# State-space and expert layer: a chunk's products as 64x64 quadrants, y's channels reordered, three of eight gathered pieces without the add

## The chip, the cores and the metric

One core of a Trainium2 chip runs the whole kernel in one launch. The metric is the device time in microseconds (us), from profiled and unprofiled executions of the same program.

## What is computed

The input x has 32 sequences of 256 tokens, 128 channels (8192 tokens). Every token is normalised to xn, and the output is `x + ssm(xn) + ffn(xn)`.

- `ssm` projects xn to 256 hidden channels, mixes them by a gate with a convolution of three tokens, and runs a linear recurrence with 16 states per channel along the sequence: `state = A_d * state + B_d * u_t`, `y_t = sum(state * C)`. Then `out = y @ W_out.T + b_out`, and the result is a layer norm of `xn + out` with gain and offset.
- `ffn` is a mixture of eight experts (128 to 512 to 128, relu). Each token goes to two neighbouring experts, and the two outputs are averaged.

## The kernel before, in words

All engines run programs written out by hand, joined by semaphores. The order is: statistics and normalising; projections, while GpSimd (POOL) scatters the tokens to DRAM in expert order; 37 tiles of 256 sorted tokens through two experts each, their outputs stored in `ys_dram`; the state-space loop; the output projection with the last layer norm. The change touches the last two stages and one small thing at the start.

**State-space loop** (TensorE, L1277 to L1316; VectorE, L1096 to L1104; ScalarE, L707 to L724). The recurrence is cut into chunks of Q = 32 tokens, 256 chunks in all. One group g holds four hidden channels, whose 4 x 32 tokens are the 128 partitions; the 256 chunks are the columns. 64 groups (32 for each half `hb` of the hidden channels) are taken as 32 pairs r, and two pairs make a duo q; there are 16 duos (`NDUO`). For a duo PE runs three phases of fp32 matmuls:

- `inject(q + 1)` (L1287): what each chunk adds to the 64 states of a group, a 128x64 weight, 224 columns, four matmuls; the two groups of a pair (`ab`) go to PSUM partitions 0 to 63 and 64 to 127 of bank `q % 2`.
- the products inside the chunk (L1307): a 128x128 weight `INTRA[:, g, :]`, 256 columns, four matmuls. This weight is block diagonal, four blocks of 32x32, one for each channel; the rest is zero.
- the read-out of the states (L1313): 64 rows by 128 columns, 256 columns, four matmuls, accumulated on the products inside. It waits for the scan of the duo on VectorE (`s_scan`, L1102).

The scan needs `inject`, and the decay rows that ScalarE writes (`decay`, L712). ScalarE moves each pair's result from two PSUM banks to SBUF over the inputs u (L723). Six banks hold three pairs. In the second half of the loop (q from 8, `DPB`) VectorE also transposes the finished first half of y after each scan, in eight pieces of 1024 tokens (`y_piece(0, n)`, L1093; `YT[0]` is `RC[:, 1, :]`).

**Output stage.** After the last duo VectorE runs `y_piece(1, 0)` and `y_piece(1, 1)`, and then a written-out sequence over 16 groups of 512 tokens: `stats`, `scale_batch`, `y_piece(1, n)`, `gain(n)` (L1138) and `add_base(n)` (L1143) for the eight pieces n; after `add_base(n)` SP stores piece n (L462). PE projects y with `WoT` (L1328), whose rows have to be in the channel order of y's partitions.

**Gathers.** `add_base(n)` adds `GA[n]`, which is x plus the expert outputs in token order. SP first loads x into `GA[n]` (`load_x`, L434); POOL waits for it and issues eight indirect DMAs of 128 rows each with an add at the destination (L548). `GA[0..3]` lie in `AR`, which is free once the experts are done; `GA[4..7]` lie over `INTRA`'s first half and are loaded after pair 16. Their order on POOL is n = 0 to 7, 64 DMAs in all:

```python
for n in range(NB8):
    pool.wait_ge(s_xg[n], 16)
    for t in range(TB8):
        nc.gpsimd.indirect_dma_start(out=GA[n][:, t, :], out_offset=None, in_=ys_dram,
            in_offset=..., compute_op=ALU.add).then_inc(s_gat[n], 16)
```

At the start ScalarE's queue loads the weights (`WRAW`), and PE transposes the eight tiles of them (L1176), the two of W_out last.

Of the kernel before, what the change touches and what calls it, by code (L numbers as in the profile page):

```python
# [23 lines left out]
def ssm_moe_layer(nc, x, W_x, b_x, W_g, b_g, conv_w, conv_b, A_raw, B_ssm, C_ssm, W_dt, b_dt,  # L24
# [30 lines left out]
    with ExitStack() as ctx:  # L55
# [130 lines left out]
        WRAW = carve(RC1, (3 * HB + HB) * D).rearrange("p (j d) -> p j d", d=D)  # L186

# [31 lines left out]

        lng_b = lng[:, :].rearrange("p (o d) -> p o d", o=1).broadcast_to([P, TB8, D])  # L220
# [25 lines left out]
        s_step2 = sem("sync_steps")  # L246
        s_fg = sem("last_scaled")
        s_fp = sem("last_group_normalised_vector")
        s_xnd = sem("normalised_tokens_stored")
        s_xg = [sem(f"x_below_outputs_{n}") for n in range(8)]  # L250
        s_actl = sem("last_log_ready")
        s_wt = sem("weights_transposed")
        s_wh = sem("weights_high_ready")
# [97 lines left out]
        def _(sp):  # L351
# [82 lines left out]
            def load_x(n):  # L434
                sp.dma_start(GA[n], x_v[:, n * TB8:(n + 1) * TB8, :]).then_inc(s_xg[n], 16)
# [31 lines left out]
        def _(pool):  # L467
# [22 lines left out]

            for q in range(QT):
# [50 lines left out]

            pool.wait_ge(s_yst, bounds[E] * 16 + 16)
            pool.sem_inc(s_step, 1)
            for n in range(NB8):
                pool.wait_ge(s_xg[n], 16)
                for t in range(TB8):
# [3 lines left out]
                                                 compute_op=ALU.add).then_inc(s_gat[n], 16)  # L551
# [191 lines left out]
        def _(dve):  # L743
# [329 lines left out]
            for ab in range(2):  # L1073
                for q in range(NQ):
                    src = slice(Q * q, Q * (q + 1))
                    dst = slice(Q * (2 * ab + q // 2), Q * (2 * ab + q // 2 + 1))
                    V.tensor_scalar(READ[dst, :, q * Q:(q + 1) * Q], RT[src, ab, :, 0:Q], half[src, q % 2:q % 2 + 1], None,
                                    ALU.mult)
# [16 lines left out]

            dve.wait_ge(s_m2, bounds[E])  # L1096
            for q in range(NDUO):
# [5 lines left out]
                if q >= DPB:  # L1103
                    y_piece(0, q - DPB)  # L1104
            dve.wait_ge(s_ytr, NYP)
# [34 lines left out]
            def add_base(n):  # L1140
                dve.wait_ge(s_fg, n + 1)
                dve.wait_ge(s_gat[n], 16 * TB8)
                V.tensor_tensor(VV[n], VV[n], GA[n], ALU.add).then_inc(s_fo, 1)  # L1143
# [25 lines left out]
        def _(pe):  # L1169
# [4 lines left out]
            for n in range(4 * HB):  # L1174
                bank = n // 4 if n < 3 * HB else 3
                T.transpose(ps[bank][:, (n % 4) * P:(n % 4 + 1) * P], WRAW[:, n, :], identity[:, :]).then_inc(s_wt, 1)  # L1176
# [100 lines left out]
            def inject(q):  # L1277
# [3 lines left out]
                for k in range(2):  # L1281
                    for ab in range(2):
                        g = 4 * dp + 2 * k + ab
                        u = UT[hb][:, g, :].rearrange("p (b c) -> p b c", c=NC)[:, :, 0:NC - 1]
                        dst = ps[q % 2][64 * ab:64 * ab + 64, k * BC:(k + 1) * BC].rearrange(
                            "p (b c) -> p b c", c=NC)[:, :, 1:NC]
                        ins = T.matmul(dst, INJ[:, hb * NG + g, :], u, start=True, stop=True)  # L1287
                ins.then_inc(s_inj, 1)

            def out_bank(r, ab):  # L1290
# [68 lines left out]
```

## Time and profile before

| | us |
|---|---|
| median of 3 runs | 517.13 (516.88 to 517.64) |
| the profiled execution | 516.79 |
| its span, first to last instruction | 515.0 |
| PE busy | 440.5 (86%) |
| VectorE (DVE) busy | 405.0 (79%) |
| ScalarE (ACT) busy | 319.0 (62%) |
| POOL busy | 280.3 (54%) |
| granted TensorE clock, mean | 0.978 of full speed |

The profiled execution lasts 1.8 us longer than its span. Busy shares are averages over stages whose limits differ; which wait ended last in a stage is read from the chain and the timeline. In the rows, a span of PE is modelled at its end, so PE is read by the starts of its instructions. An fp32 matmul leaves two records.

### The profile page before, as it was taken

The page shows a single profiled execution, that of the slowest core. Times are in us where ns is not written, and L with a number is a line of the kernel's source. Part 1 is how long each engine was busy: PE and PEld are TensorE (multiplying, and loading weights), DVE is VectorE, ACT ScalarE, POOL GpSimd, SP SyncE. Part 2 cuts the span into 40 slices and gives each one's busy share as a digit, 9 for nine tenths or more (in the row PEclk, how much of TensorE's full clock was granted, in tenths as well). Part 3 has the DMA queues.
Part 4 walks back from the last instruction along what each step waited for, and adds up shares of the span by engine and source line. Part 5 has one row for each costly group of instructions (what it writes and reads, how often), then busy time and mean ns, then how long its engine had stood idle before and what let it go on. Part 6 is the DMA issues. An engine that isn't in the chain of part 4 may idle for free.

```text
span 515.0 us, 10344 instructions
## 1 busy us (share of the span) xinstructions
PE 440.5 (86%) x3199; PEld 389.5 (76%) x3199; DVE 405.0 (79%) x699; ACT 319.0 (62%) x818; POOL 280.3 (54%) x269
## 2 busy tenths in 40 slices
PE   1006999998899999999998898999999999798850
PEld 1005778876899999999998897999986666586640
DVE  6988899995999999999998899960022388379984
ACT  1393999999777777776667566565555544134460
POOL 2297777774233232324531655632218888888884
PEclk9999999999999999999999999999999999899975
DMA  9997545534111111113112142211136395834555
GB/s 240 271 390 232 175 154 156 173 121 145 35 39 41 41 41 41 41 41 82 45 41 64 44 124 85 59 42 41 41 99 127 42 290 103 196 41 78 112 113 142
DMA packets 87507, 56.48 MB, mean 110 GB/s; under 512 B 6162, under 2 KB 81978, under 8 KB 87482
## 3 DMA queue, kind: packets, MB, share of 16 engines
q1 hardware_dynamic: 75258, 47.27, 31.1%
q0 software_dynamic: 11264, 8.40, 9.3%
q10 hardware_dynamic: 960, 0.52, 0.4%
q8 instruction: 10, 0.16, 0.1%
q14 instruction: 15, 0.12, 0.1%
HBM read 27.99 MB, written 23.99 MB: 101 GB/s over the span
## 4 chain that ended last, share of the span: by engine, by line
issue 44%; POOL 33%; DMA 11%; DVE 4%; PE 2%; POOLq 2%; ACT 2%; SPq 0%; ACTq 0%; DVEq 0%
POOL RB L548 10%; POOL AR L548 10%; DMA sorted_tokens<-RA,posi 8%; POOL AR L538 6%; POOL sorted_tokens L508 4%; DMA RA<-in_L_attn_x_dram 2%; DVE RC L786 2%; PE PS L1269 1%; ACT RA L574 1%; POOL b2p L529 1%; POOL b2p L524 1%; POOLq L345 1%; DMA RB<-sorted_outputs,posi 1%; DMA AR<-in_L_attn_x_dram 1%; POOL XT L514 1%
## 5 line engine op out<-in xcount | busy, mean ns | idle before, releaser
L1269 PE MATMUL PS<-AR 128*128 128x128 f32 x1184 | 138.4, 275 | 2.2 <-ACT AR L692 2.2
L1269 PEld LDWEIGHTS PS<-AR 128*128 128x128 f32 x1184 | 135.1, 192 | 2.7 <-ACT AR L692 2.7
L692 ACT ACTIVATE AR<-PS,VC 128x256 f32<-128x256 f32 x296 | 112.1, 489 | 11.2 <-PE PS L1254 11.2
L1252 PE MATMUL PS<-XT,RR 128*128 128x256 f32 x296 | 86.4, 292 | 7.9 <-POOL RR L534 3.1
L514 POOL TENSOR_TENSOR XT<-XTF,XT 128x256 fp32r<-128x256 f32 x37 | 37.7, 1018 | 100.1 <-ACT XT L664 100.1
L1254 PE MATMUL PS<-XT,RR 128*128 128x256 f32 x296 | 82.8, 280 | 0.0
L1253 PE MATMUL PS<-XT,RR 128*128 128x256 f32 x296 | 82.6, 279 | 0.0
L508 POOL DMA_INDIRECT sorted_tokens<-RA,posi x64 | 62.3, 974 | 21.1 <-issue 12.3
L538 POOL TENSOR_TENSOR AR<-AR,b2p 128x256 f32<-128x256 f32 x37 | 34.9, 942 | 54.0 <-ACT AR L701 53.8
L1252 PEld LDWEIGHTS PS<-XT,RR 128*128 128x128 f32 x296 | 55.8, 188 | 9.5 <-POOL RR L534 3.5
L701 ACT ACTIVATE AR<-PS 128x128 f32<-128x128 f32 x74 | 16.5, 275 | 70.6 <-PE PS L1269 67.6
L548 POOL DMA_INDIRECT RB<-sorted_outputs,posi x32 | 53.5, 1673 | 9.7 <-issue 9.7
L548 POOL DMA_INDIRECT AR<-sorted_outputs,posi x32 | 49.5, 1546 | 15.2 <-issue 9.4
L1253 PEld LDWEIGHTS PS<-XT,RR 128*128 128x128 f32 x296 | 55.8, 188 | 0.0
L1254 PEld LDWEIGHTS PS<-XT,RR 128*128 128x128 f32 x296 | 55.6, 188 | 0.0
L1208 PE MATMUL PS<-RR 128*128 128x512 f32 x96 | 40.8, 425 | 0.7 <-DVE RR L836 0.7
L1210 PE MATMUL PS<-RR 128*128 128x512 f32 x96 | 38.4, 400 | 0.0
L1209 PE MATMUL PS<-RR 128*128 128x512 f32 x96 | 38.4, 400 | 0.0
L494 POOL TENSOR_SCALAR RA<-RA,mean,rstd 128x128 f32<-128x128 f32 x21 | 17.2, 831 | 18.7 <-DVE nmr L806 18.7
L891 DVE SCALAR_TENSOR_TENSOR AR<-PS,VC,AR 128x512 f32<-128x512 f32 x32 | 24.0, 751 | 3.7 <-DVE AR L887 0.2
L1328 PE MATMUL PS<-WoT,RA 128*128 128x128 f32 x128 | 26.1, 287 | 0.0
L1328 PE MATMUL PS<-WoT,RC 128*128 128x128 f32 x128 | 26.0, 287 | 0.0
(233 smaller groups left out, 926.7 us busy)
## 6 DMA issues: line engine op xcount, KB each, us to landing
sorted_tokens<-RC SPq DMA_DIRECT2D x8, 640.0 KB, 6.9
AR<-sorted_tokens SPq DMA_DIRECT2D x39, 128.0 KB, 2.1
sorted_outputs<-AR SPq DMA_DIRECT2D x37, 128.0 KB, 1.8
RA<-in_L_attn_x_dram SPq DMA_DIRECT2D x8, 512.0 KB, 7.7
AR<-RA SPq DMA_DIRECT2D x16, 256.0 KB, 2.4
normalised_tokens<-RA SPq DMA_DIRECT2D x16, 256.0 KB
RB<-normalised_tokens SPq DMA_DIRECT2D x8, 512.0 KB, 6.8
out_dram<-RB SPq DMA_DIRECT2D x8, 512.0 KB, 3.2
```

Source lines behind the costliest of these rows:

```text
L508: nc.gpsimd.indirect_dma_start(out=xs_dram, in_=XN[:, t, :], in_offset=None, out_offset=bass.IndirectOffsetOnAxis(ap=posi[:, t:t + 1], axis=0)
L514: nc.gpsimd.tensor_tensor(XT[:, FT:2 * FT], XTF[:, :], XT[:, 0:FT].bitcast(F32), ALU.subtract).then_inc(s_xlo, 1)
L538: nc.gpsimd.tensor_tensor(YSB, YSB, b2p[:, :].rearrange("p (o d) -> p o d", o=1).broadcast_to([P, FH, D]), ALU.add).then_inc(s_yad, 1)
L548: nc.gpsimd.indirect_dma_start(out=GA[n][:, t, :], out_offset=None, in_=ys_dram, in_offset=bass.IndirectOffsetOnAxis(ap=posi[:, n * TB8 + ...
L692: nc.scalar.activation(HID[n][:, k, :], ps[2 * n + k // 2][:, (k % 2) * FT:(k % 2 + 1) * FT], ACT.Relu, bias=B1C[:, e, k:k + 1]).then_inc( ...
L1208: T.matmul(bank, PW[:, 0, n, :], xh[s], start=True, stop=False)
L1209: T.matmul(bank, PW[:, 0, n, :], xl[s], start=False, stop=False)
L1252: T.matmul(bank, W1h[slot][:, w], XT[:, 0:FT], start=True, stop=False)
L1253: T.matmul(bank, W1h[slot][:, w], XT[:, FT:2 * FT], start=False, stop=False)
L1254: T.matmul(bank, W1l[slot][:, w], XT[:, 0:FT], start=False, stop=True).then_inc(s_m1[n], 1)
L1269: ins = T.matmul(ps[5 + h][:, 0:D], HID[n][:, k, h * P:(h + 1) * P], W2S[slot][:, k, :], start=(n == 0 and k == 0), stop=(n == 1 and k == ...
L1328: T.matmul(vpsum(t), YT[hb][:, t * P:(t + 1) * P], WoT[:, hb, :], start=False, stop=False)
```

## The change

1. INTRA is used by its two diagonal 64x64 blocks alone. A group's product inside the chunk becomes two matmuls (w = 0, 1) with 64 rows and 64 columns of weights. The row half w chooses the PSUM bank, the group `ab` chooses the partitions within it. A duo has eight of them, not four.
2. So that the read-out still lands on them, the states and y are reordered: `inject` becomes eight matmuls of 32 weight columns each for a duo, not four of 64; READ and A32 are built with other destinations (as many instructions); the read-out of 64x128 goes by w.
3. `WOP` holds W_out with its columns in y's new order. POOL makes it with two strided copies of 128x128 at the start, and PE waits for it before its last two weight transposes.
4. Pieces 0, 1 and 2 are gathered without an add (`bypass`), into `GA[n]`, with no wait for x. Their x goes to `XB[n]`, the last three pieces of `YT[0]`. VectorE adds it with `add_x(n)`, after the scans of duos 8, 11 and 14; `y_piece(0, 5)` to `y_piece(0, 7)` wait for these adds.
5. POOL waits for the end of the experts and for `s_mat` by itself, before its first gather. A few semaphore steps are added.

```diff
+            pool.wait_ge(s_wraw, 64)
+            for hb in range(HB):
+                nc.gpsimd.tensor_copy(WOP[:, hb, :].rearrange("p (a m w) -> p a m w", a=2, w=2),
+                                      WRAW[:, 3 * HB + hb, :].rearrange("p (w m a) -> p a m w", w=2, a=2)).then_inc(s_wpm, 1)
...
+            pool.wait_ge(s_m2, bounds[E])
...
+            pool.wait_ge(s_xs, bounds[E] * 16 + 32)
...
             pool.wait_ge(s_yst, bounds[E] * 16 + 16)
...
+            pool.wait_ge(s_mat, 1)
             for n in range(NB8):
-                pool.wait_ge(s_xg[n], 16)
+                if n >= NPL:
+                    pool.wait_ge(s_xg[n], 16)
...
-                                                 compute_op=ALU.add).then_inc(s_gat[n], 16)
+                                                 compute_op=ALU.bypass if n < NPL else ALU.add).then_inc(s_gat[n], 16)
...
+            def add_x(n):
+                dve.wait_ge(s_gat[n], 16 * TB8)
+                dve.wait_ge(s_xg[n], 16)
+                V.tensor_tensor(GA[n], GA[n], XB[n], ALU.add).then_inc(s_xb, 1)
...
                 if q >= DPB:
+                    if q - DPB >= NYP - NPL:
+                        dve.wait_ge(s_xb, q - DPB - (NYP - NPL) + 1)
                     y_piece(0, q - DPB)
+                if q >= DPB and (q - DPB) % 3 == 0 and (q - DPB) // 3 < NPL:
+                    add_x((q - DPB) // 3)
...
-                        dst = ps[q % 2][64 * ab:64 * ab + 64, k * BC:(k + 1) * BC].rearrange(
-                            "p (b c) -> p b c", c=NC)[:, :, 1:NC]
-                        ins = T.matmul(dst, INJ[:, hb * NG + g, :], u, start=True, stop=True)
+                        for w in range(2):
+                            r0 = 64 * w + 32 * ab
+                            dst = ps[q % 2][r0:r0 + 32, k * BC:(k + 1) * BC].rearrange(
+                                "p (b c) -> p b c", c=NC)[:, :, 1:NC]
+                            ins = T.matmul(dst, INJ[:, hb * NG + g, 32 * w:32 * w + 32], u, start=True, stop=True)
...
-                        T.matmul(out_bank(r, ab), INTRA[:, hb * NG + g, :], UT[hb][:, g, :], start=True, stop=False)
+                        for w in range(2):
+                            h = slice(64 * w, 64 * w + 64)
+                            T.matmul(out_bank(r, w)[64 * ab:64 * ab + 64, :], INTRA[h, hb * NG + g, h], UT[hb][h, g, :],
+                                     start=True, stop=False)
```

## Rows read from the trace of the kernel before

**Rows 1.** The page, part 4: the chain that ended last, by line.
```profile
POOL RB L548 10%; POOL AR L548 10%; DMA sorted_tokens<-RA,posi 8%; POOL AR L538 6%; POOL sorted_tokens L508 4%; DMA RA<-in_L_attn_x_dram 2%; DVE RC L786 2%; PE PS L1269 1%; ACT RA L574 1%; POOL b2p L529 1%; POOL b2p L524 1%; POOLq L345 1%; DMA RB<-sorted_outputs,posi 1%; DMA AR<-in_L_attn_x_dram 1%; POOL XT L514 1%
```

**Rows 2.** Timeline, POOL, 386 to 507: start us, us, operation, [idle before <-releaser].
```profile
386.15 1.65 POOL L548 DMA_INDIRECT AR<-sorted_outputs,posi  x1 [5.74 <-DMA AR<-in_L_attn_x_dram]
...
445.36 1.54 POOL L548 DMA_INDIRECT RB<-sorted_outputs,posi  x1 [0.30 <-issue]
...
489.14 2.19 POOL L548 DMA_INDIRECT RB<-sorted_outputs,posi  x1 [0.30 <-issue]
...
506.25 2.09 POOL L548 DMA_INDIRECT RB<-sorted_outputs,posi  x1 [0.30 <-issue]
```

**Rows 3.** Chain of waits, last 15 us: start us, us, what.
```profile
506.25 3.84 DMA RB<-sorted_outputs,posi
```

**Rows 4.** Timeline, DVE, first transposes of y's second half, and the end.
```profile
441.33 3.73 DVE L1093 STREAM_TRANSPOSE RA<-RC 128x1024 f32<-128x1024 f32 x2 [3.05 <-ACT RC L723]
...
488.74 1.18 DVE L1143 TENSOR_TENSOR RB<-RB,AR 128x1024 f32<-128x1024 f32 x1
...
505.70 1.22 DVE L1138 TENSOR_TENSOR RB<-RB,lng 128x1024 f32<-128x1024 f32 x1
510.18 1.23 DVE L1143 TENSOR_TENSOR RB<-RB 128x1024 f32<-128x1024 f32 x1 [3.26 <-DMA RB<-sorted_outputs,posi]
```

**Rows 5.** Timeline, ACT, one duo, and the last evictions.
```profile
386.51 1.09 ACT L723 ACTIVATE RA<-PS 128x512 f32<-128x512 f32 x2 [2.02 <-PE PS L1313]
387.48 0.90 ACT L712 ACTIVATE RAWX<-cmask,A 128x256 f32<-128x256 bf16 x2
...
440.14 1.08 ACT L723 ACTIVATE RC<-PS 128x512 f32<-128x512 f32 x2 [1.90 <-PE PS L1313]
```

**Rows 6.** Timeline, PE, one duo of the state-space loop.
```profile
390.72 0.98 PE L1287 MATMUL PS<-RA,RB 128*64 128x224 f32 x8
391.63 1.99 PE L1307 MATMUL PS<-RA,RB 128*128 128x256 f32 x8
393.55 1.13 PE L1313 MATMUL PS<-AR,RB 64*128 64x256 f32 x8
394.62 0.98 PE L1287 MATMUL PS<-RA,RB 128*64 128x224 f32 x8
```

**Rows 7.** Windows, PE, line L1313 alone: us, busy (x records), PEclk, DMA share, GB/s.
```profile
393.54:393.60 0.06, 0.05 (x2) 1.00 0.00 0
393.86:393.90 0.04, 0.04 (x4) 1.00 0.00 0
```

**Rows 8.** Timeline, DVE, 411 to 416, the loop's second half.
```profile
411.00 1.96 DVE L1093 STREAM_TRANSPOSE RC<-RA 128x1024 f32<-128x1024 f32 x1 [1.83 <-ACT RA L723]
412.89 1.18 DVE L1102 TENSOR_TENSOR_SCAN AR<-RAWX,PS 128x512 f32<-128x512 f32 x1
413.99 1.95 DVE L1093 STREAM_TRANSPOSE RC<-RA 128x1024 f32<-128x1024 f32 x1
415.85 1.19 DVE L1102 TENSOR_TENSOR_SCAN AR<-AR,PS 128x512 f32<-128x512 f32 x1
```

**Rows 9.** Timeline, SP's queue, around the end of the experts.
```profile
382.10 1.88 SPq L435 DMA_DIRECT2D AR<-in_L_attn_x_dram  x3
```

**Rows 10.** Timeline, POOL, plain scatter of line L508.
```profile
81.95 0.96 POOL L508 DMA_INDIRECT sorted_tokens<-RA,posi  x1 [0.30 <-DMA sorted_tokens<-RA,posi]
83.21 0.95 POOL L508 DMA_INDIRECT sorted_tokens<-RA,posi  x1 [0.30 <-issue]
```

**Rows 11.** DMA by queue: packets, MB, share; 40 to 125 us, the scatter.
```profile
q0 software_dynamic: 2048, 4.20, 14.9%
```

**Rows 12.** The same view of 376 to 515 us, the gathers.
```profile
q0 software_dynamic: 9216, 4.20, 25.3%
```

**Rows 13.** Timeline, start of the kernel, PE.
```profile
9.55 1.94 PE L1176 MATMUL PS<-identity,RC 128*128 128x128 f32 x8 [9.55 <-DMA RC<-in_L_attn_W_out_dram]
```

**Rows 14.** Timeline, start of the kernel, POOL.
```profile
16.11 1.59 POOL L494 TENSOR_SCALAR RA<-RA,mean,rstd 128x128 f32<-128x128 f32 x2 [11.74 <-DVE nmr L806]
```

## What the change does to the time: the prediction

> **What bounds the kernel now.** I began with the page's chain of waits, which says what ended last and not what was busy most. From 386 us on, nearly all of it is POOL on line L548: the gathers into AR and RB hold 10% of the span each [rows 1]. POOL's timeline shows why. The first gather starts at 386.15, after 5.74 us of waiting for x; the 33rd starts at 445.36 and the 64th at 506.25 [rows 2]. So one gather takes 1.85 us in the first half and 1.96 in the second. The last one lands 3.84 us after its issue, at 510.09 [rows 3].
>
> The second question is how far behind the next engine is. VectorE ended `gain(7)` at 505.70 + 1.22 = 506.92 and then idled 3.26 us for that landing, before `add_base(7)` at 510.18 [rows 4]. POOL therefore holds only 3.3 us. If gathers alone became cheaper, the gain would stop there. From `add_base(7)`'s start to the span's end it is 515.0 - 510.18 = 4.8 us, of which 1.2 is the add and the rest the last store.
>
> VectorE's own chain hangs on the state-space loop. Its output stage starts with the transposes at 441.33, after 3.05 us of waiting for ScalarE's last eviction [rows 4], which followed PE's last read-out [rows 5]. From 441.33 to 506.92 it is 65.6 us, in which no row of VectorE shows a wait for a gather. In the loop PE never idles: inject starts at 390.72, the products inside at 391.63, the read-out at 393.55, the next inject at 394.62 [rows 6]. A duo takes 0.91 + 1.92 + 1.07 = 3.90 us; ScalarE works 1.09 + 0.90 us of it [rows 5].
>
> **The change, part by part.** *Products inside a chunk.* Four full-array matmuls (eight records) take 1.92 us; the four read-outs, in which two 64-row halves run side by side, take 1.07 with as many columns. 
>
> *Inject.* It goes from four matmuls to eight, in four column strips of 32. Four at once: 0.91 as now. Two at a time: four more slots of 224 columns, 4 x 0.21 x 224/256 = +0.74. I take 0.91, with 0.74 as the dear end; it must not gain, as its columns streamed per strip are the same. The read-out has the same shapes: 1.07. PE's duo comes to 0.91 + 1.07 + 1.07 = 3.05.
>
> *The loop's first half.* ScalarE needs 1.99 of those 3.05, and the scan follows decay by far more than a duo ahead of its read-out, so PE sets the pace. The first transpose waits for eviction 16 and starts now at 411.00 [rows 8]; eight duos make that 411.00 - 8 x 0.85 = 404.2.
>
> *The second half.* Now VectorE has a scan and a transpose per duo, 412.89 to 415.85, 1.10 + 1.86 = 2.96 us [rows 8], hidden under 3.90; under 3.05 it is barely hidden, and `add_x` comes on top. An add of this size took 1.2 us [rows 4]. What is queued behind it is the next scan, for which PE's read-out waits. From 404.2 to the end of scan 15: seven transposes 13.0, seven scans 7.7, three adds 3.6, so 428.5. PE alone would bring its last read-out from 439.4 (0.75 before the eviction of 440.14) to 439.4 - 13.6 = 425.8; VectorE is late by 2.8. Read-out at 428.6, evictions 0.75 later for 1.08 [rows 5], transposes at 430.5: 10.8 us earlier than 441.33. The new waits for `s_xb` cost nothing, since each add precedes its transpose by at least a scan.
>
> *The gathers.* The plain ones do not wait for x. They wait for what SP waits for too, and SP issued at 382.10 [rows 9], so about 382.2 and not 386.15: 3.95 earlier. What a plain gather costs POOL the trace does not show. The nearest rows are the plain scatter of as many rows, one per 83.21 - 81.95 = 1.26 us [rows 10], and the adding gather, 1.85. Below 1.26 I exclude nothing, but it would gain nothing, as will be seen. I take 1.26: the queue's packets point to the add as the difference. The 64 scatters made 2048 packets of 2 KB, the 64 gathers 9216 of half a KB, for the same 4.20 MB [rows 11, 12]. Whether the add or the direction splits them stays open. Then 24 x 1.26 = 30.2 gives 412.4, and 39 intervals of 1.85 to 1.96 put the last issue at 484.6 to 488.8 and its landing, 3.84 later, at 488.4 to 492.7. The adds have their pieces in time: piece 2 lands near 416, and is wanted at about 425; even at 1.85 it would come about 430, 5 us late.
>
> *Two things beside each other.* A gather beside an add on VectorE takes longer, 2.19 and not 1.54 at 489.14, where L1143 ran from 488.74 [rows 2, 4]. Three new adds cost POOL 3 x 0.65 = 2.0 us, so a landing at 490.4 to 494.7. The Trainium skill ("SBUF — State Buffer", Who interferes with whom) says that VectorE and GpSimd share a port pair as a lock, the later one blocked until the first ends. By that rule an add could cost POOL its whole 1.2 us, 3.6 in all, and the landing could be as late as 496.3, still at VectorE's time within 0.2; the row shows about half of that.
>
> *The output stage* is unchanged: 65.6 us from 430.5 is 496.1 for `add_base(7)`, behind POOL's landing by 1.4 to 5.7. Late is now VectorE alone, which is busy for nearly all of the stage. Span 496.1 + 4.8 = 500.9.
>
> *Start of the kernel.* W_out is there when PE starts at 9.55 [rows 13]; POOL is idle from about 4.4 until 16.11 [rows 14]. Two strided copies, at 0.8 us each like the POOL operations of that size in [rows 14] or at twice that for their strides, end by 12.8, and no one wants the last transposes before 16. Cost zero; without that cover, at most 3.2 us. The waits and steps added on POOL and PE are in the tenths.
>
> **Sum.** The profiled execution: 516.8 with a span of 515.0. New span 500.9, 14.1 less, so 502.7. The median of the runs, 517.13, lies 0.3 above the profiled one, and so I put 503.0. A difference under 0.2% (1.0 us) can hardly be told from none.
>
> **Rivals.** *Slower: only two tiles at a time.* The products inside stay at 1.92 and inject grows by 0.74: a duo of 4.64, 16 x 0.74 = 11.9 us more. Transposes at 453.2, `add_base(7)` at 518.8, 525.7 with the same 0.3. The cheaper gathers can't help, because VectorE's chain sets the end. It turns slower as soon as a duo grows by 3.3 / 16 = 0.2 us. For it: no row shows more than two tiles at once, and PE would have to take 16 pairs of weights and records where eight go by in 0.91. Against it: the pairwise starts [rows 7]. The Trainium skill states the rule behind this rival ("TensorE: Matmul & The Clock Gate", The mechanism): matmuls start and end in program order, however many tiles there are. With both records of an fp32 matmul side by side in the program, only neighbours could overlap, two at a time, and the time would be this rival's. By that rule, though, the first record of L1313 would start alone; [rows 7] show two. So the trace speaks against it, unless the records are interleaved before they reach the engine. 14%.
>
> *A plain gather costs as much as an adding one.* 64 gathers as now, but from 382.2: last issue at 502.3, 2.0 more for the adds, landing at 508.1, and the time is 514.8 + 0.3 = 515.1. POOL becomes the end again from a plain gather of about 1.49 us. For: the direction is that of the gathers. Against: the packets. 11%.
>
> *Inject runs two strips at a time, the products four.* A duo of 3.79; PE's last read-out 16 x 0.11 = 1.8 earlier, not 10.8; 512.0. The same place covers a dearer VectorE or a gather between the ends, 507 to 513. 11%.
>
> **How the numbers follow.** The forecast has 62% and spans 500 to 506 (adds or gathers somewhat dearer, or a phase start of PE somewhat cheaper). The range 499.5 to 515.5 takes in the second and third rival, 84% together; it leaves out the slower one. Faster by over 0.2%: 62 + 11 + 11, 0.84. Slower 0.14. Same 0.02, where two effects happen to cancel.
>
> **What would show it.** In the new profile: L1307 as 64x64 records, four started within a few hundredths of a us, and its phase near 1.07 us; inject still near 0.91; duos of 3.05 in the first half, idle of PE in the second with VectorE as releaser; transposes at about 430.5; 24 gathers 1.26 us apart from 382.2; VectorE with no wait for a gather at the end. Wrong would be a PE that never idles with duos of 3.9 or more, a chain that still ends in POOL, or 24 gathers at 1.85.

## The result, and the profile after

The changed kernel takes **504.27 us** (median of 4 runs, 503.87 to 504.45), beside 517.38 (516.88 to 517.83) for the kernel before in the same session: a ratio of 0.974 [0.973, 0.976], 13.1 us less. The forecast was 503.0, with a range of 499.5 to 515.5. The profiled execution took 504.45 with a span of 502.7. This holds for the chips on which the kernel before takes 517 to 518 us. On one on which it takes 592 us the change makes the kernel slower by 4%, which the fourth experiment shows.

The page of the changed kernel, part 1 and part 4 (the chain that ended last, by engine):

```profile
PE 429.0 (85%) x3455; PEld 376.7 (75%) x3455; DVE 406.1 (81%) x702; ACT 319.3 (64%) x818; POOL 264.4 (53%) x271
...
issue 35%; PE 19%; DVE 17%; POOL 12%; DMA 11%; ACT 3%; POOLq 2%; SPq 0%; DVEq 0%; ACTq 0%
```

The gathers (L548 before, L566 now), 10% and 10% of the chain in [rows 1], are no longer among the lines of the chain that the page names; POOL's share of it falls from 33% to 12%. PE is busy 11.5 us less (440.5 before), though it now has 3455 records; POOL is busy 15.9 us less. VectorE is busy 1.1 us more. The busy sums alone would not have told that the span falls by 12.3; what changed is which waits end last.

**PE in the loop.** Timeline of PE in the changed kernel; read-out (L1352), inject (L1322), products inside (L1345), and below them the first matmul of the output stage. Read the starts.

```profile
385.00 1.13 PE L1352 MATMUL PS<-AR,RB 64*128 64x256 f32 x8
386.06 0.96 PE L1322 MATMUL PS<-RA,RB 128*32 128x224 f32 x16
386.96 1.10 PE L1345 MATMUL PS<-RA,RB 64*64 64x256 f32 x16
387.98 1.14 PE L1352 MATMUL PS<-AR,RB 64*128 64x256 f32 x8
...
433.13 0.59 PE L1363 MATMUL PS<-bop,first 128*128 128x512 bf16 x1 [2.80 <-issue]
```

A duo is 387.98 - 385.00 = 2.98 us, where [rows 6] gave 3.90. The products take 1.02 and not 1.92, inject takes 0.90 with twice the records, the read-out 1.06. Windows of line L1345 alone (us, busy and records of PE and of PEld, clock, DMA share, GB/s) show how the phase opens:

```profile
386.95:387.00 0.05, 0.04 (x4) 0.04 (x4) 1.00 0.55 164
```

Four records have started within 0.05 us, where [rows 7] have two within 0.06.

**VectorE.** Timeline of VectorE in the changed kernel: the first scan, the start of the second half, the end of the loop, the end of the kernel.

```profile
380.74 1.22 DVE L1125 TENSOR_TENSOR_SCAN AR<-AR,PS 128x512 f32<-128x512 f32 x1 [5.49 <-ACT AR L730]
...
404.76 1.97 DVE L1111 STREAM_TRANSPOSE RC<-RA 128x1024 f32<-128x1024 f32 x1 [0.92 <-ACT RA L741]
406.66 1.18 DVE L1117 TENSOR_TENSOR AR<-AR,RC 128x1024 f32<-128x1024 f32 x1
407.75 1.21 DVE L1125 TENSOR_TENSOR_SCAN AR<-RAWX,PS 128x512 f32<-128x512 f32 x1
...
426.84 1.17 DVE L1117 TENSOR_TENSOR AR<-AR,RC 128x1024 f32<-128x1024 f32 x1
...
431.13 3.70 DVE L1111 STREAM_TRANSPOSE RA<-RC 128x1024 f32<-128x1024 f32 x2 [0.17 <-ACT RC L741]
438.87 0.89 DVE L1140 BATCH_NORM_STATS2 FST<-PS 128x6 f32<-128x128 f32 x4 [4.04 <-PE PS L1368]
...
497.85 1.23 DVE L1173 TENSOR_TENSOR RB<-RB 128x1024 f32<-128x1024 f32 x1
```

From 404.76 on, scan, transpose and `add_x` follow each other with no idle time (VectorE is busy for 16.96 of the 17 us from 414 to 431, PE for 13.33); the wait of 3.05 us ahead of the transposes of y's second half [rows 4] is 0.17 now. Those transposes start at 431.13, 10.2 us earlier. The last `add_base` (L1173) starts at 497.85, 12.3 us earlier, and shows no wait: the 3.26 for the gather [rows 4] is gone. VectorE now sets the end.

**The gathers.** Timeline of POOL: the copies of W_out, the 1st and the 19th gather (both plain), those beside the three `add_x` (407.31, 417.74, 427.06), the last one. From the 1st to the 19th it is 22.53 us, 1.25 for each.

```profile
9.45 0.64 POOL L500 COPY RC<-RC 128x128 f32<-128x128 f32 x2 [5.07 <-DMA RC<-in_L_attn_W_out_dram]
...
383.52 1.00 POOL L566 DMA_INDIRECT AR<-sorted_outputs,posi  x1 [2.18 <-DMA sorted_outputs<-AR]
...
406.05 0.95 POOL L566 DMA_INDIRECT AR<-sorted_outputs,posi  x1 [0.30 <-issue]
407.31 1.35 POOL L566 DMA_INDIRECT AR<-sorted_outputs,posi  x1 [0.30 <-issue]
...
417.74 1.63 POOL L566 DMA_INDIRECT AR<-sorted_outputs,posi  x1 [0.30 <-issue]
...
427.06 2.37 POOL L566 DMA_INDIRECT AR<-sorted_outputs,posi  x1 [0.30 <-issue]
...
488.75 1.62 POOL L566 DMA_INDIRECT RB<-sorted_outputs,posi  x1 [0.30 <-issue]
```

A gather that starts while one of these adds runs takes longer by what is left of the add, less 0.12 us. The third `add_x` ends at 426.84 + 1.17 = 428.01, 0.95 after the gather's start at 427.06, and the gather takes 0.83 more than 1.54. At 407.31 it is 0.53 left and 0.41 more; at 417.74, beside the add just below, 0.22 and 0.09; and in [rows 2, 4] 0.78 and 0.65. So it is in nine profiles for all 111 gathers that start during an add or a gain of this size: what is left of it, less 0.10 to 0.14. The gather waits for VectorE's operation to end. In the other order neither is longer: the gather at 453.75 takes 1.54 and the gain's multiplication (L1165) that starts at 453.86 takes 1.23. Beside scans, transposes and statistics the gathers keep their usual time, but for a few hundredths (the one at 406.05 beside a transpose takes 0.95).

```profile
416.79 1.17 DVE L1117 TENSOR_TENSOR AR<-AR,RC 128x1024 f32<-128x1024 f32 x1
```

The DMA queues between 376 and 503 us (packets, MB, share), beside 9216 packets in [rows 12]:

```profile
q0 software_dynamic: 6528, 4.20, 21.8%
```

64 adding gathers made 9216, so 144 each, and 64 plain scatters 2048 [rows 11], so 32 each. 24 gathers at 32 and 40 at 144 make 6528 exactly. So it is the add that splits a gather's rows into packets of half a KB, not the direction.

**Two stretches that differ without being touched.** The expert stage: the window of 319 to 323 us, first the kernel before, then the changed one (the columns are time, busy and records of PE, PEld, DVE, ACT, POOL, then clock, DMA share, GB/s).

```profile
319.00:323.00 4.00, 3.23 (x28) 3.23 (x29) 3.92 (x8) 2.11 (x6) 1.44 (x3) 1.00 0.16 48
```

```profile
319.00:323.00 4.00, 3.49 (x17) 3.50 (x18) 3.92 (x9) 1.37 (x4) 1.14 (x2) 0.57 0.21 62
```

And the start of the output stage, nearly the same 10 us relative to the transposes, before (441.33) and after (431.13):

```profile
440.00:450.00 10.00, 7.20 (x43) 5.54 (x40) 4.62 (x6) 1.08 (x2) 8.48 (x6) 0.83 0.98 234
```

```profile
430.00:440.00 10.00, 7.20 (x34) 5.55 (x31) 5.55 (x7) 1.03 (x2) 8.47 (x6) 0.66 0.98 237
```

With two levels, full and half, a mean of 0.83 over 10 us is 3.4 us at 1.2 GHz, and 0.66 is 6.8 us. PE had been idle for 2.80 us just before its first matmul of the stage, in both kernels (433.13 in the changed one, 443.33 before). Before, all 3.4 us lie behind that matmul; in the changed kernel 5.7 of the 6.8 do. The wait for the first projected group is 4.04 us and was 2.89, which is the 1.1 by which the output stage grew. The expert stage's stretch costs some 0.9 us (the first scan is at 380.74; the row of before, just below, has 379.80).

```profile
379.80 1.22 DVE L1102 TENSOR_TENSOR_SCAN AR<-AR,PS 128x512 f32<-128x512 f32 x1 [5.48 <-ACT AR L712]
```

Neither stretch's length belongs to the changed kernel. A second profile of it (`changed_third`, experiment 6), a faster execution of 502.65 us, has no such stretch in the expert stage and its first scan at 379.88. There 3.5 us at half clock lie behind PE's first matmul, the first transposes of y's second half are at 430.43, and the last `add_base` is at 496.04, so that the output stage takes 65.6 us:

```profile
496.04 1.23 DVE L1173 TENSOR_TENSOR RB<-RB 128x1024 f32<-128x1024 f32 x1
```

### The profile page after: what moved, and what is told of

Read it like the earlier page. It is cut to its first block, busy times and chain, and to the rows that moved or that the text cites. A ratio compares the mean times of both kernels' runs of the same rounds, so it can differ in the third digit from the quotient of the medians.

```text
span 502.7 us, 10867 instructions
## 1 busy us (share of the span) xinstructions
PE 429.0 (85%) x3455; PEld 376.7 (75%) x3455; DVE 406.1 (81%) x702; ACT 319.3 (64%) x818; POOL 264.4 (53%) x271
## 4 chain that ended last, share of the span: by engine, by line
issue 35%; PE 19%; DVE 17%; POOL 12%; DMA 11%; ACT 3%; POOLq 2%; SPq 0%; DVEq 0%; ACTq 0%
DMA sorted_tokens<-RA,posi 9%; PE PS L1302 6%; POOL AR L550 5%; POOL sorted_tokens L520 4%; DVE RC L1111 2%; DVE FST L1140 2%; DMA RA<-in_L_attn_x_dram 2%; PE PS L1352 2%; PE PS L1367 2%; PE PS L1285 2%; PE PS L1287 2%; PE PS L1286 2%; DVE RB L1165 2%; DVE RC L804 2%; DVE AR L1125 2%
## 5 line engine op out<-in xcount | busy, mean ns | idle before, releaser
L1285 PEld LDWEIGHTS PS<-XT,RR 128*128 128x128 f32 x296 | 56.4, 191 | 9.2 <-POOL RR L546 3.5
L1286 PEld LDWEIGHTS PS<-XT,RR 128*128 128x128 f32 x296 | 56.4, 191 | 0.0
L566 POOL DMA_INDIRECT RB<-sorted_outputs,posi x32 | 51.2, 1600 | 9.8 <-issue 9.8
L1287 PEld LDWEIGHTS PS<-XT,RR 128*128 128x128 f32 x296 | 56.3, 190 | 0.0
L566 POOL DMA_INDIRECT AR<-sorted_outputs,posi x32 | 36.5, 1139 | 11.6 <-issue 9.4
```

The lines of the kernel that those rows point to most:

```text
L1285: T.matmul(bank, W1h[slot][:, w], XT[:, 0:FT], start=True, stop=False)
L1286: T.matmul(bank, W1h[slot][:, w], XT[:, FT:2 * FT], start=False, stop=False)
L1287: T.matmul(bank, W1l[slot][:, w], XT[:, 0:FT], start=False, stop=True).then_inc(s_m1[n], 1)
```

## The experiments

Theory: products in quadrants shorten VectorE's chain, plain gathers shorten POOL's, and only both together bring the 13 us. Rivals: PE's gain comes from pairs only, or needs a certain order; one of the parts does all of it.

### 1. The parts alone

Quadrants, new channel order, but all gathers with the add:

```diff
-        NPL = 3
+        NPL = 0
```

> The changed kernel with all eight pieces gathered by the adding DMA and no add on VectorE (the quadrants and the new channel order stay). My theory: 64 adding gathers at 1.85 to 1.96 us end where they ended before, so POOL sets the end again and nearly all of what the quadrants bring in the loop is idle time of VectorE before its last add: 516 to 518.5 us, with the y transposes at 427 to 430 us and about 15 us of waiting for the last gather. A rival, that the loop's shortening is worth itself at the end (12 us or so) whatever POOL does, says 505 to 508.

Measured: 518.55 us (517.6 to 520.59, 10 runs), ratio 1.0022 [1.0005, 1.0038] to 517.72 for the kernel before, at the upper end of the theory's range. VectorE, then the chain's last link:

```profile
427.00 3.74 DVE L1111 STREAM_TRANSPOSE RA<-RC 128x1024 f32<-128x1024 f32 x2 [0.36 <-ACT RC L741]
...
495.43 1.23 DVE L1173 TENSOR_TENSOR RB<-RB 128x1024 f32<-128x1024 f32 x1 [6.89 <-DMA RB<-sorted_outputs,posi]
...
510.99 1.23 DVE L1173 TENSOR_TENSOR RB<-RB 128x1024 f32<-128x1024 f32 x1 [13.20 <-DMA RB<-sorted_outputs,posi]
```

```profile
507.61 3.28 DMA RB<-sorted_outputs,posi
```

The loop is faster than in the changed kernel itself, as there is no `add_x` in it: transposes at 427.00. All of that, 14.3 us, comes back in two waits for gathers, 6.89 and 13.20 us; together they are 20.1, since they also hold the 3.26 that was there before and what the stage saves elsewhere (without its waits it takes 63.9 us, not 65.6, with PE's clock at full at its start). POOL's chain alone sets the end. Its last gather lands at 510.89, 0.8 later than before, and that is the small loss that is left.

The gathers and `add_x` as changed, with the matmuls of before (two places, set against the kernel before):

```diff
-                                                 compute_op=ALU.add).then_inc(s_gat[n], 16)
+                                                 compute_op=ALU.bypass if n < NPL else ALU.add).then_inc(s_gat[n], 16)
...
+                if q >= DPB and (q - DPB) % 3 == 0 and (q - DPB) // 3 < NPL:
+                    add_x((q - DPB) // 3)
```

> The kernel before with only the gathers changed: three pieces gathered plainly, their x added by VectorE in the loop; full-array products, old channel order. My theory: POOL ends near 493 us, VectorE's chain is as before because three adds of 1.1 us fit under PE's duos of 3.90 us, so only the 3.3 us come off by which VectorE waited for the last gather: 513.5 to 514.5 us. The rival, that adds and transposes in the loop's second half push it, says 515 to 517 us.

Measured: 513.47 us (511.94 to 515.26, 5 runs), ratio 0.992 [0.989, 0.995]. VectorE:

```profile
441.29 3.70 DVE L1106 STREAM_TRANSPOSE RA<-RC 128x1024 f32<-128x1024 f32 x2 [2.84 <-ACT RC L736]
```

Here PE paces the loop, so the three adds fit into VectorE's idle time and the transposes start where they did (441.33 in [rows 4]). What is gained is the wait at the end: the last `add_base` starts at 508.16 and waits for no gather. That wait was 3.3 us and the medians differ by 4.2, where the runs of this kernel alone spread over 3.3. Alone the parts bring nothing and 4 us; together they bring 13. Each is bounded by the chain that the other shortens.

### 2. The order of the quadrants

The eight products of a duo go tile by tile, so that four records in a row of the program belong to one tile. The loop over k keeps its waits and ends ahead of them:

```diff
-                    for ab in range(2):
-                        g = 4 * dp + 2 * k + ab
-                        for w in range(2):
+                for ab in range(2):
+                    for w in range(2):
+                        for k in range(2):
+                            r = 2 * q + k
+                            g = 4 * dp + 2 * k + ab
```

> The changed kernel with the eight products inside a chunk of a duo issued tile by tile: both matmuls of one 64x64 tile, then both of the next, so that four records in a row are for one tile. If PE takes matmuls strictly in program order and only neighbours on different tiles overlap, a tile's four records run one after another: about 13 slots of 0.215 us instead of 4, a phase of 2.9 us instead of 1.02, duos near 4.9 us and 525 us or more. If each tile takes its records from the queue by itself, the phase stays at 1.0 to 1.1 us and the time within 0.5 us of the changed kernel, 503.5 to 505.

Measured: 504.99 us (503.32 to 506.05, 4 runs), ratio 0.974 [0.971, 0.977]. Timeline of PE, then the window at the phase's start, L1347 alone:

```profile
385.43 1.13 PE L1354 MATMUL PS<-AR,RB 64*128 64x256 f32 x8
...
387.38 1.11 PE L1347 MATMUL PS<-RA,RB 64*64 64x256 f32 x16
388.43 1.14 PE L1354 MATMUL PS<-AR,RB 64*128 64x256 f32 x8
```

```profile
387.37:387.43 0.06, 0.05 (x4) 0.05 (x4) 1.00 0.71 60
```

The duo is 3.00 us, the phase 1.05, and four records start within 0.06 us, though by the program's order the first four share a tile, where they could only follow each other: one after the other, four slots of 0.2 us would be gone before a second tile began. Records of different tiles don't wait for each other's turn here. The rule of the Trainium skill that the prediction weighed ("TensorE: Matmul & The Clock Gate", The mechanism) would have made this order by far the worst; neither it nor the changed kernel bears it out for fp32 records of 64x64 tiles.

### 3. TensorE busy ahead of the output stage

Nine bf16 matmuls (128x128 weights, 512 columns; 2.1 us in all) are issued while VectorE transposes y's second half; their results are overwritten.

```diff
             pe.wait_ge(s_yev, NPAIR)
+            for n in range(9):
+                T.matmul(ps[7].rearrange("p (t d) -> p t d", d=D), first[:, :], ..., start=True, stop=True)
```

> The changed kernel with nine more matmuls of 128x512 bf16 into a free PSUM bank while PE waits for the first transposes of the output stage (their results are overwritten). In the changed kernel PE idled from 430.3 to 433.1 us and its granted clock was 0.5 from 432.0 to 438.8. My theory: that clock delays VectorE's first statistics by about 2.9 us, so with the clock kept at 1.0 the time falls by 1.5 to 3 us, to 501.5 to 502.8. The rival, that the first output groups wait for something else (loads of normalised tokens) or that VectorE's later chain absorbs it, says 504 to 505.

Measured: 503.31 us (501.13 to 505.34, 4 runs), ratio 0.973 [0.970, 0.977]; the profiled execution, the fastest of them, has a span of 499.4. The window, and VectorE:

```profile
430.00:440.00 10.00, 9.56 (x63) 7.10 (x64) 6.56 (x12) 0.39 (x1) 8.36 (x6) 1.00 1.05 243
```

```profile
430.49 3.77 DVE L1111 STREAM_TRANSPOSE RA<-RC 128x1024 f32<-128x1024 f32 x2 [0.17 <-ACT RC L741]
435.56 0.89 DVE L1140 BATCH_NORM_STATS2 FST<-PS 128x6 f32<-128x128 f32 x4 [1.29 <-PE PS L1371]
...
494.53 1.23 DVE L1173 TENSOR_TENSOR RB<-RB 128x1024 f32<-128x1024 f32 x1
```

The clock stays at full, the wait for the first projected group is 1.29 and not 4.04, and the stage takes 494.53 - 430.49 = 64.0 us instead of 66.7. The stage's length, from these transposes to VectorE's last `add_base`, goes with the time at half clock behind PE's first matmul: none and 64.0 here, 3.4 and 65.6 before, 3.5 and 65.6 in the second profile, 5.7 and 66.7 in the first. So the mechanism is there in the traces. The median lies between the theory's 501.5 to 502.8 and the rival's 504 to 505, and the runs of this and of the changed kernel (504.27, in another session) overlap: a gain in the time is not shown.

### 4. Another chip

The next four ran on a chip on which the kernel of before takes 592.31 us (589.28 to 595.21, 11 runs). The chips on which it takes 517 to 518 are called ordinary here.

> The changed kernel itself, so that the other runs of this call have it on the same chip. 503.5 to 505 us; the share of it that varies from run to run should be in how long the clock stays at 0.5 near 432 us (3.4 or 6.8 us).

Measured: 617.9 us (617.11 to 618.85, 6 runs), ratio **1.043 [1.039, 1.046]**: here the change is slower. Windows of the changed kernel there, in the scatter and in the first half of the loop:

```profile
58.00:136.00 78.00, 14.38 (x34) 9.57 (x35) 7.18 (x14) 8.37 (x17) 49.51 (x52) 0.50 0.17 58
464.00:504.00 40.00, 16.54 (x45) 5.40 (x44) 1.22 (x1) 2.77 (x6) 31.28 (x28) 0.54 0.33 72
```

PE does 34 records in 78 us, where the ordinary chip shows 390 in the same stretch; in the loop it does 45 in 40 us. POOL is undisturbed. The loop in detail, PE and then POOL:

```profile
474.05 0.53 PE L1322 MATMUL PS<-RA,RB 128*32 128x224 f32 x1 [1.53 <-issue]
...
486.07 0.58 PE L1345 MATMUL PS<-RA,RB 64*64 64x256 f32 x1 [1.45 <-issue]
488.87 0.58 PE L1345 MATMUL PS<-RA,RB 64*64 64x256 f32 x1 [2.22 <-issue]
```

```profile
474.08 0.94 POOL L566 DMA_INDIRECT AR<-sorted_outputs,posi  x1 [0.30 <-issue]
475.33 0.94 POOL L566 DMA_INDIRECT AR<-sorted_outputs,posi  x1 [0.30 <-issue]
```

PE issues single records, most of them 0.7 to 2.8 us apart, and waits for nothing that the profile shows, while POOL goes on with a plain gather every 1.25 us. Set beside the ordinary chip by VectorE's milestones: the first scan is at 456.24 and not 380.74, 75.5 us later; from there to the first transposes of the second half it is 63.3 us and not 24.0, another 39.3; from there to the end it is 97.5 and 97.9. Both stalls begin while POOL issues indirect DMAs without an add, back to back, and outlast them: the plain gathers run from 459.04 to 488.75, the single records of PE from about 464 to 500, beside the first adding gathers too. The other 32 adding gathers, from 530.65 on, go out back to back with no stall. The kernel of before has the first of these stretches, but in the loop only adding gathers, and it is 592.31 - 517.38 = 74.9 us slower on this chip, as much as the first stall by itself. That fits plain gathers as what brings the second one; it is argued from the sums, since no trace of the kernel of before was taken on this chip, and a kernel with quadrants and adding gathers was not run there, so that a part of the quadrants in the second stall is not excluded. What holds PE back inside the stall is open too.

> The changed kernel with the three adds of x moved out of the state-space loop: x is loaded over the last three pieces of the other half of y, once the transposes of the first half are done, and the adds follow the statistics of output groups 0, 2 and 4, where VectorE waits for PE in two of the three places. My theory: VectorE sets the pace of the loop's second half only through the adds; without them the transposes start at 427.5 to 428.5 us and not at 431.1, of which one add of 1.1 us is paid later: 501.5 to 502.8 us. The rival, that VectorE with a scan and a transpose (2.96 us) sets the pace by itself, or that the late loads of x delay the normalised tokens, says 503.5 us or more.

> Adds later and nine matmuls of 128x512 bf16 that keep PE busy before the output stage. If the two gains are on one chain one after the other they add up: 499 to 501 us, unless POOL's last gather (landing at 492 to 493 us) becomes the end again; its bound is 492.6 + 4.8 + 1.8 = 499.2 us, and this run should come close to it. If they do not add, 501.5 or more.

> The changed kernel with inject as four matmuls of 64 weight columns for a duo and not eight of 32. The states then land in the old order, so the read-out mixes channels and y is not the reference's; all else has the same shapes. My theory: four column strips at once cost what two did, so the phase stays at 0.89 to 0.91 us and the time at 503.5 to 505 us. If the eight cost more than four (a slot more would be 0.19 us a duo, 1.5 us in the loop's first half), this run is faster than the changed kernel by that: 502 to 503 us.

These three expected times of the ordinary chip. On this one they took 615.32 (614.19 to 617.65), 612.84 (611.44 to 613.82) and 616.33 us (614.02 to 619.05), ratios 1.039, 1.034 and 1.039. Against the changed kernel's 617.9 there, the medians of the first two are 2.6 and 5.1 lower, though runs of the first overlap with the changed kernel's; the third can't be told from it. The edits and the repeats stand below.

### 5. Inject alone as before

Its four matmuls of 64 columns instead of eight of 32. Inject's rows then belong to other states than the read-out takes, so the output differs; as much work is done.

```diff
-                        for w in range(2):
-                            r0 = 64 * w + 32 * ab
...
+                        dst = ps[q % 2][64 * ab:64 * ab + 64, k * BC:(k + 1) * BC].rearrange(
+                            "p (b c) -> p b c", c=NC)[:, :, 1:NC]
+                        ins = T.matmul(dst, INJ[:, hb * NG + g, :], u, start=True, stop=True)
```

> The inject product alone in four matmuls of 64 columns, as in the kernel of before, the products in quadrants; the inject then gives other values. Theory: the inject phase costs its 0.89 to 0.91 us in either form (on the other chip 0.91 against 0.89), so that 503.5 to 505 us is left, the same as the changed kernel. Rival (the inject in four column strips is a gain of its own, hidden in the 2.98 us of a duo): the phase takes over 1.0 us and the kernel 507 us or more.

This repeat met another chip on which the kernel of before is slow (592.53 us, 590.25 to 593.41): 613.51 us (612.34 to 616.01), ratio 1.036 [1.033, 1.038]. The changed kernel was not run on it, so the time says little of inject; that this variant is slower than the kernel of before there too is all that the second such chip adds. But the phase can be read. Timeline of PE, past the stall:

```profile
535.61 0.98 PE L1320 MATMUL PS<-RC,RB 128*64 128x224 f32 x8
536.52 1.09 PE L1343 MATMUL PS<-RC,RB 64*64 64x256 f32 x16
```

0.91 us for the eight records of 64 columns, 0.90 for the sixteen of 32. Sixteen records take no longer than eight, so four strips run at once, and inject's split is free.

### 6. The adds later

The base pieces 0, 1 and 2 get x after the statistics of groups 0, 2 and 4 and not between the transposes of the loop. Their x goes to the last pieces of RA, loaded once the first half's transposes are done.

```diff
-        XB = [batch(RC[:, 1, :], NB8 - NPL + n) for n in range(NPL)]
+        XB = [batch(RA[:, :], NB8 - NPL + n) for n in range(NPL)]
...
-                if q >= DPB and (q - DPB) % 3 == 0 and (q - DPB) // 3 < NPL:
-                    add_x((q - DPB) // 3)
...
                 ins = stats(g)
+                if g in (0, 2):
+                    add_x(g // 2)
...
+                if g == 4:
+                    add_x(2)
```

It ran on an ordinary chip (before: 518.36 us, 517.86 to 519.3, 9 runs), with the changed kernel and with both edits together (the adds later and the nine matmuls of experiment 3).

> The changed kernel once more, beside the two below, since their comparison before stood on a chip on which the kernel of before itself took 592 us. Theory: on a chip where the kernel of before takes 517 us this takes 503.5 to 505 us, and the stalls of 88 and 39 us seen on the other chip, both in stretches in which GpSimd issued its gathers and scatters, are absent. Rival (the stalls belong to the changed kernel): it is over 515 us again.

Measured: 503.71 us (502.65 to 506.53, 5 runs), ratio 0.973 [0.971, 0.976]. No stall; the first result repeats. The 88 us in this expectation is too much for the first stall on the other chip: by the first scan it is 75.5.

> The three gather targets get x after the statistics of groups 0, 2 and 4 and not between the transposes. Theory (three adds of 1.2 us on VectorE ahead of the statistics are paid in full when VectorE sets the pace to the end, but moving them keeps their sum on VectorE): y(1,.) transposes start some 1 to 2 us sooner, the end gains only what VectorE idled before the statistics, 501.5 to 503.5 us. On the other chip it stood 2.6 us under the changed kernel. Rival: the adds were hidden in VectorE's gaps of the loop, and moving them out makes it slower, 505 to 508 us.

Measured: **500.24 us** (499.53 to 502.52, 5 runs), ratio 0.965 [0.963, 0.968]. VectorE:

```profile
405.22 1.96 DVE L1114 STREAM_TRANSPOSE RC<-RA 128x1024 f32<-128x1024 f32 x1 [0.92 <-ACT RA L744]
...
428.25 3.74 DVE L1114 STREAM_TRANSPOSE RA<-RC 128x1024 f32<-128x1024 f32 x2 [0.36 <-ACT RC L744]
433.31 0.89 DVE L1139 BATCH_NORM_STATS2 FST<-PS 128x6 f32<-128x128 f32 x4 [1.32 <-PE PS L1373]
434.12 1.21 DVE L1120 TENSOR_TENSOR AR<-AR,RA 128x1024 f32<-128x1024 f32 x1
...
493.93 1.23 DVE L1172 TENSOR_TENSOR RB<-RB 128x1024 f32<-128x1024 f32 x1 [1.01 <-DMA RB<-sorted_outputs,posi]
```

The loop's second half takes 428.25 - 405.22 = 23.0 us, not 26.4: the three adds, at 1.1 us each, are out of it. The output stage takes 493.93 - 428.25 = 65.7 us, with three adds in it and a new wait of 1.01 for the last gather. That is no more than the changed kernel's 65.6 and 66.7, but those had PE at half clock for a while at the stage's start, and here the clock is at full. Beside a stage at full clock (64.0 in experiment 3) it is 1.7 more: the wait of 1.0, and 0.7 for adds that are 3.3 us of work. The rest fills time in which VectorE waits for PE's first groups. The expectation had kept their sum on VectorE and was too dear by over 1 us. Why the clock stays up here after the same 2.80 us of idle time of PE is not shown.

> The adds later and the nine small matmuls ahead of the output stage. Theory: with TensorE's granted clock kept at full in the first output products the two gains add, 499.5 to 501.5 us, 3 to 5 us under the changed kernel (on the other chip 5.1 us), and the end is then set by GpSimd's gathers or VectorE alike. Rival: only one of the two counts, since both end in the same wait of VectorE, 501.5 to 503.5 us.

Measured: 499.21 us (499.17 to 500.69, 5 runs), ratio 0.964 [0.963, 0.966]. VectorE:

```profile
403.94 1.97 DVE L1114 STREAM_TRANSPOSE RC<-RA 128x1024 f32<-128x1024 f32 x1 [0.92 <-ACT RA L744]
...
492.57 1.23 DVE L1172 TENSOR_TENSOR RB<-RB 128x1024 f32<-128x1024 f32 x1 [0.91 <-DMA RB<-sorted_outputs,posi]
```

The median is just under the range of the theory, but the reason it gave fails and the rival's holds: from the first transposes to the last `add_base` it is 88.6 us here and 88.7 with the adds alone. The nine matmuls add nothing, since the clock of the adds-later kernel is at full in that stretch without them; the two profiles differ by the 1.3 us by which the loop started earlier, and the runs of the two kernels overlap. Both now end in a wait for POOL of about 1 us. VectorE's chain and POOL's are as good as level, and this is the best version found, 4.5 us under the changed kernel, of which the adds alone bring 3.5.

## Why the prediction was right

**The forecast's own case came about**, and the time lies 1.3 us above the forecast. Its steps in order:

- *Products inside, 1.07 us.* Measured 1.02, four tiles at once. The argument from pairwise starts [rows 7] held, and the rival of two tiles is refuted, by the changed kernel and by the order tile by tile. The rows had shown no more than two tiles at once, so four was a guess with an argument behind it.
- *Inject 0.91, read-out 1.07, a duo 3.05.* Measured 0.90, 1.06, 2.98. The third rival falls.
- *First transposes 404.2.* Measured 404.76, of which 0.94 is the later start of the loop: from the first scan, 0.4 shorter than forecast.
- *VectorE sets the pace after that, 26.3 us to the second half's transposes.* Measured 431.13 - 404.76 = 26.4. The adds cost 1.10 each there, not 1.2. VectorE does not idle, PE does.
- *Plain gather every 1.26 us.* Measured 1.25. The packets had pointed the right way, and the second rival falls. Its turning point of 1.49 was given too far off: by the prediction's own landing, 1.4 to 5.7 us ahead of VectorE, 24 gathers could cost 1.32 to 1.50 before POOL sets the end.
- *POOL's start at 382.2.* Measured 383.52: 0.94 for the late loop, and 0.4 because it waited for the last store of the experts (2.18 us of idle time), which I had put together with SP's wait.
- *A gather beside an add costs 0.65 more.* The three took 1.35 instead of 0.94, 1.63 instead of 1.54, and 2.37 instead of 1.54: 0.4, 0.1 and 0.8 more, 1.3 together where I had 2.0. The price is not fixed: it is what is left of the add when the gather starts, less 0.12. The prediction read its row as half of an add, but only 0.78 us of that add were left, and the gather waited for nearly all of them. The Trainium skill's rule of a lock ("SBUF — State Buffer", Who interferes with whom), by which the later one is blocked until the first ends, agrees with these rows where the add is first; where the gather is first, they show no wait (453.75 and 453.86 above). The same section infers that a `tensor_tensor` does not hold up POOL's writing of the DMA's descriptors, the orders for the DMA engines; the measured 0.83 of 0.95 us speaks against that.
- *Copies at the start cost nothing.* They run at 9.45, and POOL then idles 5.90 us.
- *Output stage 65.6 us.* Measured 497.85 - 431.13 = 66.7. This is the term that was furthest off. I took the stage over whole, and with it the 3.4 us at half clock in it; they became 6.8, 5.7 of them while PE worked. In the second profile it is 65.6. The prediction also said that VectorE is busy for nearly all of the stage; in the kernel before it is busy for 53.9 of these 65.6 us, and for 8.3 of the first 14.7.

The sum: 496.1 forecast for the last `add_base`, 497.85 measured, 1.75 more: + 0.94 for the loop's late start, - 0.3 within the loop, + 1.1 in the output stage. The two that are late come from stretches at 1.2 GHz on parts that the change doesn't touch, and the second profile is late by neither: its last `add_base` is at 496.04 and its span 500.9, within 0.1 of the forecast. How near the forecast comes is thus partly luck, since the executions of the changed kernel differ by up to 3.9 us (502.65 to 506.53); that it lies in the right place is not.

**What I did not see** is in no step: that the sign depends on the chip. The times of before all came from an ordinary one, and nothing in its trace pointed to stalls beside indirect DMAs. The range holds for chips like the one that it was read from (504.27 and 503.71 us) and not for the one of experiment 4 (617.9).

I also left the placing of the adds unquestioned. The prediction priced them at 3.6 us on a VectorE that sets the pace, and that price was nearly right (3.3); the next sentence should have asked where VectorE still waits afterwards. The output stage opens with such waits, and moving the adds there is worth 3.5 us.

## What to carry to other kernels

Where two chains end within a few us of each other, price a change on one of them at the gap to the other, and look for the pair: here the parts brought 0 and 4 us alone and 13 together. A block-diagonal fp32 weight used by its two 64x64 blocks took 1.02 us where the whole had taken 1.92, in both orders of the blocks that were tried. An indirect DMA on POOL that starts during a two-input add on VectorE waits for the add's end; one that is under way when the add starts does not. Work that must be added to the engine that sets the pace goes where that engine still waits for another; and a change in how POOL's DMAs go out should be timed on more than one chip.

## What the hardware showed that I had not expected

- The same kernel of before takes 517 to 518 us in three sets of runs and 592 in two others, on other chips. No chip stands in more than one set, so that the chip can't be told from its state at the time. In the stalls PE, ScalarE and VectorE nearly stand still (34 records of PE in 78 us), while POOL issues its indirect DMAs at the usual 1.26 or 1.25 us.
- Sixteen fp32 records on four tiles take some 0.2 us for each four, an estimate by the prediction's slots from the phase's 1.02 us, also when the program lists them tile by tile (3.00 beside 2.98 us for a duo).
- An indirect DMA of 128 rows with an add costs POOL 1.54 us and makes 144 packets, without it 0.94 us and 32 packets.
- A gather of 0.94 or 1.54 us that starts during a two-input fp32 add on VectorE takes longer by the rest of the add less 0.12 us (0.41 of 0.53, 0.83 of 0.95, 0.65 of 0.78).
- The clock fell to half for 3.4 us in one execution and for 6.8 in the next at the same place, after the same 2.80 us of idle time of PE, and not at all in two others with the same idle time (adds later, quadrants only).
